# Expert queue: row number and expert change of two tiles packed in one word for SyncE, landing waits grouped, padding tiles counted as no change

## The chip, the cores and the metric

The kernel runs on one core of one Trainium2 chip. The metric is device time in microseconds (us), the median of several executions. A profiled execution comes with it: its span runs from the first to the last instruction of the program.

## The reference

A small language-model tower over 8 sequences of 512 tokens, 256 channels. The last of its three parts is the one that the change touches.

```python
h = _L0_tok_ref(x, ...)                       # embedding, depthwise convolution of 31 taps
h = h + _L0_attn_ref(_layernorm(h), ...)      # linear attention, 16 heads
h = h + _L0_ffn_ref(_layernorm(h), ...)       # 8 experts, 4 of width 256 and 4 of width 512, top 2

# inside _L0_ffn_ref
topw, sel = jax.lax.top_k(jax.nn.sigmoid(xf @ router_w.T), 2)
h = jnp.square(jax.nn.relu(jnp.einsum('td,edw->tew', xf, W1e)))
y = jnp.einsum('tew,ewd->ted', h, W2e)
out = jnp.einsum('ted,te->td', y, combine)
```

Each token goes to two experts, and the two weighted results are added to its row of the output.

## The kernel before

The routing step writes each token's row (256 channels, weight, token number) twice into `queue_d`, a queue in HBM that has a stretch of rows for every expert. When all are counted, VectorE works out a table over tiles of 128 rows: 71 tiles (`TILES`), the experts of width 512 first. Experts have whole numbers of tiles, so that some rows of a last tile, and all rows of the last tiles of the table (padding tiles), are filler rows, which add to 128 spare rows of the output.

**The expert loop** (function `experts`) goes through the tiles in order. Tile j takes these steps:

- SyncE (SP) loads the tile's rows from HBM into one of 8 slots (`load`, L1712 to L1715). It reads the row number from the table with a register load (`value_load`, L1710).
- TensorE turns the rows (L1849), multiplies by the first weights (L1859), turns the squared activations (L1875) and multiplies by the second weights (L1859). ScalarE (ACT) and VectorE (DVE) take the results out of PSUM in between: x_hi L1760, x_lo L1805, relu L1765, act_w L1817, a_hi L1771, a_lo L1823.
- ScalarE takes the result to `y` (`take_y`, L1777), one of 4 buffers (`RING`). Before it writes, the add of tile j - 4 from the same buffer must have landed. ScalarE works in order: while this instruction waits, all that comes after it waits.
- SyncE allows the add (`allow`, L1717 to L1727): it waits for y, then for landings of the adds of tiles j - 3 to j - 1, and increments `may_add`. If tile j belongs to another expert than tile j - 1, these three adds must have landed, since two experts may hold the same token. If not, the waits ask for one landing fewer of each buffer, which take_y has already waited for. The number to wait for is computed in a register from `apart`, a second table of 0 or 16.
- GpSimd (POOL) waits for `may_add` and issues the add as an indirect DMA that accumulates in `out` (L1748).

All engines but SyncE and GpSimd take the loop in turns of two tiles, with a branch at the head of each on whether its oldest tile is wide (L1698): wide tiles fall through, narrow ones jump. The expert numbers are read from a word for 8 tiles (L1695). `wait_apart` (L160 to L164) is a wait followed by an increment of a semaphore, `sp_passed`, that nobody waits for.

SyncE's queue is one program in order: for tile j it first does `load(j + 8)`, then `allow(j)`, and the next tile follows.

Of the kernel before, what the change touches and what calls it, by code (L numbers as in the profile page):

```python
# [23 lines left out]
I32 = mybir.dt.int32  # L24
U32 = mybir.dt.uint32
ALU = mybir.AluOpType
# [3 lines left out]
P = 128  # L30
# [33 lines left out]
EXPERTS = 8  # L64
# [5 lines left out]
TOPK = 2  # L70
QROWS = TOKENS + P
FILLER_ROW = EXPERTS * QROWS
ROW = DIM + 2

TILES = TOKENS * TOPK // P + EXPERTS - 1
# [2 lines left out]
SLOTS = 8  # L78
TABLE = -(-TILES // SLOTS) * SLOTS
FILLERS = TABLE - TOKENS * TOPK // P  # L80
TURN = 2
RING = 4
TOTAL_W = sum(WIDTHS)
# [34 lines left out]
class Dispatch:  # L118
# [3 lines left out]
    def __init__(self, sbuf, sem):  # L122
        self.filler = sbuf("filler", [P, ROW])
        self.filler_at = sbuf("filler_at", [P, FILLERS, 2], I32)
        self.count = sbuf("count", [P, EXPERTS])
        self.count_i = sbuf("count_i", [P, EXPERTS], I32)
        self.tiles = sbuf("tiles", [P, EXPERTS])
        self.upto = sbuf("upto", [P, EXPERTS, EXPERTS])
        self.end = sbuf("end", [P, EXPERTS])
        self.end_i = sbuf("end_i", [P, EXPERTS], I32)  # L130
        self.tile_no = sbuf("tile_no", [1, TABLE])
        self.row_of = sbuf("row_of", [1, TABLE], I32)
        self.word_of = sbuf("word_of", [1, TABLE // SLOTS], I32)

        self.apart = sbuf("apart", [1, TABLE], I32)
        self.consts, self.filler_ready, self.ends_ready, self.filled, self.chain, self.ready = (sem(n) for n in (
            "table_consts", "filler_ready", "ends_ready", "filled", "table_chain", "table_ready"))

# [21 lines left out]
def wait_apart(engine, sem, value, passed):  # L160


    engine.wait_ge(sem, value)
    engine.sem_inc(passed, 1)  # L164
# [477 lines left out]
def attend(nc, ctx, sem, bank, ident, base, base0, rw_t, w1, w2, h_d, store, h_in, loaded, h_stored, raw_in,  # L642
# [48 lines left out]
    before = sbuf("before", [P, P], BF16)  # L691
# [353 lines left out]
    def vector(dve):  # L1045
# [272 lines left out]
        n = [0]  # L1318

        def chained(ins):  # L1320

            n[0] += 1
            ins.then_inc(table.chain, 1)
            dve.wait_ge(table.chain, n[0])
# [3 lines left out]
        space, at = x2_t[:].rearrange("p k n -> p (k n)"), [0]  # L1328

        def taken(rows, n):  # L1330
# [5 lines left out]
        expert_f, start_f, differs = (taken(1, TABLE) for _ in range(3))  # L1336
# [20 lines left out]
                                        ALU.mult))  # L1357
        chained(nc.vector.tensor_reduce(start_f, passed, AX, ALU.add))
        chained(nc.vector.tensor_tensor(start_f, table.tile_no[:], start_f, ALU.subtract))
        chained(nc.vector.tensor_scalar(start_f, start_f, float(P), None, ALU.mult))  # L1360
        chained(nc.vector.scalar_tensor_tensor(out=start_f, in0=expert_f, scalar=float(QROWS), in1=start_f,
                                            op0=ALU.mult, op1=ALU.add))
        chained(nc.vector.tensor_copy(table.row_of[:], start_f))

        chained(nc.vector.memset(differs[:, 0:1], 0.0))
        chained(nc.vector.tensor_tensor(differs[:, 1:], expert_f[:, 1:], expert_f[:, 0:TABLE - 1], ALU.not_equal))
        chained(nc.vector.tensor_scalar(table.apart[:], differs, 16.0, None, ALU.mult))
        chained(nc.vector.tensor_scalar(expert_f, expert_f, float(EXPERTS - 1), None, ALU.min))

        pairs = expert_f.rearrange("p (n u) -> p n u", u=2)  # L1370
        chained(nc.vector.scalar_tensor_tensor(out=word2, in0=pairs[:, :, 1], scalar=float(EXPERTS),
                                               in1=pairs[:, :, 0], op0=ALU.mult, op1=ALU.add))
        pairs = word2.rearrange("p (n u) -> p n u", u=2)
        chained(nc.vector.scalar_tensor_tensor(out=word4, in0=pairs[:, :, 1], scalar=float(EXPERTS ** 2),
                                               in1=pairs[:, :, 0], op0=ALU.mult, op1=ALU.add))
# [270 lines left out]
def experts(nc, ctx, sem, bank, ident, store, table, queue_d, out, w1_parts, w1_lo_ready, w1_zero, w2_split, queued,  # L1646
            stored):
    def sbuf(name, shape, dt=F32):
        return ctx.enter_context(nc.sbuf_tensor(name, shape, dt))
# [54 lines left out]
    def sync(sp):  # L1704
        sp.wait_ge(table.ready, 1)
        attention_left(sp)


        def row_at(j):
            return sp.value_load(table.row_of[0:1, j:j + 1], min_val=0, max_val=FILLER_ROW + (FILLERS - 1) * P)  # L1710

        def load(j, at):  # L1712
            if j >= SLOTS:
                sp.wait_ge(row_used, j - SLOTS + 1)
            sp.dma_start(rows[:, j % SLOTS], queue_d[bass.ds(at, P), :]).then_inc(rows_in[j % SLOTS], 16)  # L1715

        def allow(j):  # L1717

            sp.wait_ge(y_ready, j + 1)
            if j >= RING:  # L1720
                differs16 = sp.value_load(table.apart[0:1, j:j + 1], min_val=0, max_val=16)
            for before in range(max(0, j - RING + 1), j):
                if before < RING:
                    sp.wait_ge(added[before % RING], 16)
                else:
                    wait_apart(sp, added[before % RING], differs16 + 16 * (before // RING), sp_passed)
            sp.sem_inc(may_add, 1)  # L1727

        first_rows = [row_at(j) for j in range(SLOTS)]
        sp.wait_ge(table.filled, 16 * (EXPERTS + 3))  # L1730
        sp.wait_ge(queued, 16 * TOPK * TT * BATCHES)
        for j in range(SLOTS):
            load(j, first_rows[j])
        for j in range(TILES):
            if j + SLOTS < TILES:
                load(j + SLOTS, row_at(j + SLOTS))
            allow(j)

    def gpsimd(pool):
        attention_left(pool)  # L1740
# [202 lines left out]
```

## Time and profile before

| | us |
|---|---|
| median of 3 executions | 714.23 (714.22 to 716.38) |
| profiled execution, its own time | 714.98 |
| span of the profiled execution | 713.3 |
| first add of the expert loop starts | 500.33 |
| last of its 71 adds starts | 705.40 |

About 1.7 us of the profiled execution's own time lie outside its span. TensorE is busy for 89% of the span, GpSimd for 45%. Starts in the rows are microseconds from the start of the span. The adds are numbered 0 to 70 in order of time, so that the last one is tile 70. The idle time of an engine that is not the bound costs nothing; what matters is who ends the wait of the engine that is late.

### The profile page before, as it was taken

Reading aid. Unit: us, or ns where it says so; the run is one execution under the profiler, and the core shown is the slowest. Engines: PE = TensorE matmul, PEld = TensorE weight load, DVE = VectorE, ACT = ScalarE, POOL = GpSimd, SP = SyncE. Lnnn points to the kernel's source line nnn. Section 1 sums busy time; section 2 is a strip of 40 time slices with the busy share of each in tenths; the row PEclk is TensorE's granted clock in tenths of the full one; section 3 lists DMA queues with packets and bytes.
Section 4 is the critical chain, followed back from the end, with each engine's and each line's share of the span. In section 5 each row is a group of like instructions: output and inputs, shape, how many; then the busy total and the mean of one; then the engine's idle time right before and its main releaser. Section 6 shows DMA issues by size and latency. Waiting matters only on the chain.

```text
span 713.3 us, 15773 instructions
## 1 busy us (share of the span) xinstructions
PE 631.3 (89%) x5032; PEld 546.0 (77%) x5032; DVE 468.4 (66%) x1219; ACT 306.8 (43%) x669; POOL 321.1 (45%) x292
## 2 busy tenths in 40 slices
PE   6988479999999999999999999615999999988881
PEld 6988357788887887878878787504999999888781
DVE  6466494877879778797897866764444555554450
ACT  2560135334453353633535327422545555555551
POOL 6340351330833717427165171752354544476574
PEclk9999698999999999999999999856999999999996
DMA  6550982010111201102010020423355445576664
GB/s 225 190 124 7 230 301 62 2 59 2 61 60 39 82 1 60 60 24 97 1 61 31 17 75 3 169 93 101 62 87 80 78 76 83 79 116 108 107 100 45
DMA packets 37215, 58.11 MB, mean 81 GB/s; under 512 B 5726, under 2 KB 31066, under 8 KB 36506
## 3 DMA queue, kind: packets, MB, share of 16 engines
q1 hardware_dynamic: 21282, 35.08, 16.9%
q0 software_dynamic: 14160, 20.13, 15.7%
q10 hardware_dynamic: 1672, 1.57, 0.7%
q8 instruction: 61, 1.00, 0.6%
q14 instruction: 40, 0.33, 0.2%
HBM read 28.30 MB, written 27.42 MB: 78 GB/s over the span
## 4 chain that ended last, share of the span: by engine, by line
PE 77%; DMA 8%; DVE 6%; issue 3%; POOL 2%; ACT 1%; SPq 1%; DVEq 0%; ACTq 0%; POOLq 0%
PE bank L1427 26%; PE bank L1859 16%; PE bank L1500 7%; DMA out<-y,token_at 7%; PE bank L1470 5%; PE bank L1456 4%; PE bank L1875 2%; PE bank L1488 2%; PE bank L546 2%; PE bank L547 2%; PE bank L567 2%; PE bank L1849 2%; PE bank L529 1%; PE bank L1418 1%; PE bank L1556 1%
## 5 line engine op out<-in xcount | busy, mean ns | idle before, releaser
L1748 POOL DMA_INDIRECT out<-y,token_at x71 | 111.8, 1575 | 108.3 <-SPq L1727 107.1
L886 POOL DMA_INDIRECT queue_d<-row,slot x56 | 59.7, 1066 | 129.0 <-DVE slot L1253 114.2
L1817 DVE SCALAR_TENSOR_TENSOR act_w<-relu,queue_rows 128x512 f32<-128x512 f32 (+1 forms) x71 | 44.6, 628 | 98.2 <-ACT relu L1765 52.0
L1427 PE MATMUL bank<-xt_hi,w_first 128*128 128x512 f32 x256 | 94.8, 416 | 0.9 <-DVE second_half L1091 0.9
L1427 PE MATMUL bank<-w_first,xt_hi 128*128 128x512 f32 x256 | 84.7, 412 | 3.1 <-DVE xt_lo L1081 2.3
L877 POOL TENSOR_TENSOR second_half<-second_half,q_inv 128x512 f32<-128x512 f32 x64 | 64.9, 1042 | 42.0 <-DVE q_inv L1100 41.9
L945 ACT ACTIVATE k_exps<-bank,k_negmax 128x512 f32<-128x512 f32 x64 | 44.2, 691 | 73.8 <-DVE k_negmax L1107 73.6
L937 ACT ACTIVATE second_half<-second_half 128x512 f32<-128x512 f32 x64 | 40.3, 632 | 74.3 <-DVE second_half L1091 74.3
L1859 PE MATMUL bank<-w_hi,a_hi 128*128 x214 | 65.9, 308 | 0.8 <-issue 0.5
L1427 PEld LDWEIGHTS bank<-w_first,xt_hi 128*128 128x128 f32 x256 | 46.2, 192 | 19.6 <-issue 6.8
L1859 PE MATMUL bank<-w_lo,a_hi 128*128 x214 | 59.8, 280 | 0.0
L1859 PE MATMUL bank<-w_hi,a_lo 128*128 x214 | 59.5, 278 | 0.0
L1765 ACT ACTIVATE relu<-bank 128x512 f32<-128x512 f32 (+1 forms) x71 | 35.3, 498 | 55.6 <-PE bank L1859 55.5
L1427 PEld LDWEIGHTS bank<-xt_hi,w_first 128*128 128x128 f32 x256 | 49.2, 192 | 11.0 <-DVE second_half L1091 1.8
L1088 DVE TENSOR_REDUCE q_max<-bank 128x8 f32<-128x512 f32 x64 | 42.0, 656 | 17.6 <-PE bank L1427 17.6
L1107 DVE TENSOR_REDUCE k_negmax<-bank 128x1 f32<-128x512 f32 x64 | 42.8, 679 | 14.8 <-PE bank L1427 13.8
L1427 PE MATMUL bank<-w_first,xt_lo 128*128 128x512 f32 x128 | 50.8, 397 | 0.0
L1427 PE MATMUL bank<-xt_lo,w_first 128*128 128x512 f32 x128 | 50.7, 396 | 0.0
L1500 PE MATMUL bank<-g,wv_t 128*128 128x256 f32 x224 | 49.5, 379 | 0.0
L1859 PE MATMUL bank<-w_first,x_hi 128*128 x142 | 39.7, 361 | 9.9 <-DVE x_lo L1805 4.4
L1777 ACT ACTIVATE y<-bank 128x256 f32<-128x256 f32 x71 | 27.4, 385 | 46.1 <-PE bank L1859 29.1
L1500 PEld LDWEIGHTS bank<-g,wv_t 128*128 128x128 f32 x224 | 42.5, 190 | 6.0
(201 smaller groups left out, 1583.8 us busy)
## 6 DMA issues: line engine op xcount, KB each, us to landing
queue_rows<-queue_d SPq DMA_DIRECT2D x71, 129.0 KB, 2.1
store<-in_L_ffn_w SPq DMA_DIRECT2D x4, 1536.0 KB, 8.6
out<-res SPq DMA_DIRECT2D x8, 512.0 KB, 2.9
h_d<-store SPq DMA_DIRECT2D x6, 512.0 KB, 9.0
h_in<-h_d SPq DMA_DIRECT2D x6, 512.0 KB, 4.1
windows<-taps_d SPq DMA_DIRECT2D x4, 512.0 KB, 5.8
wqk<-in_L_attn_w_qkv SPq DMA_DIRECT2D x1, 2048.0 KB, 13.5
out<-y,token_at POOLq DMA_INDIRECT x71, 4.0
```

The costliest lines, as they stand in the source:

```text
L877: nc.gpsimd.tensor_tensor(v, v, q_inv[:, b.par, u].unsqueeze(2).to_broadcast([P, 8, DH]), ALU.mult).then_inc(q_ready, 1)
L886: pool.indirect_dma_start(out=queue_d, in_=row_of(b)[:, t, c, :], in_offset=None, out_offset=bass.IndirectOffsetOnAxis(ap=slot[:, TT * c + ...
L937: nc.scalar.activation(v, v, ACT.Exp, scale=SCALE).then_inc(q_exp_ready, 1)
L945: nc.scalar.activation(k_exps[:, c % 2], qk_bank(10 + c)[:], ACT.Exp, bias=k_negmax[:, c:c + 1], accum_out=k_sum[:, b.par, c:c + 1]).then_ ...
L1088: link(nc.vector.tensor_reduce(q_max[:, u % 2], src, AX, ALU.max), q_chain, b, Q_LINKS, 2 * u + 1 - (u > 0))
L1107: nc.vector.tensor_reduce(k_negmax[:, c:c + 1], qk_bank(10 + c)[:], AX, ALU.max, negate=True).then_inc(k_max_ready, 1)
L1427: last = nc.tensor.matmul(o, a, c, start=(n == 1), stop=(n == 3 * len(pairs)))
L1470: last = nc.tensor.matmul(tail_bank(n)[DH * r:DH * r + DH, DH * a:DH * a + DH], k[:, t, c:c + DH], q[:, b.par, t, d:d + DH], start=(t == 0 ...
L1500: last = nc.tensor.matmul(tail_bank(6)[:, DIM * kk:DIM * kk + DIM], wv_t[:, a, P * kk:P * kk + P], g[:, a], start=(a == 0), stop=(a == PAI ...
L1748: pool.indirect_dma_start(out=out, in_=y[:, j % RING, :], in_offset=None, compute_op=ALU.add, out_offset=bass.IndirectOffsetOnAxis(ap=toke ...
L1817: nc.vector.scalar_tensor_tensor(out=act_w[:, u % 2, 0:width], in0=relu[:, u % 2, 0:width], scalar=rows[:, u, DIM:DIM + 1], in1=relu[:, u ...
L1859: last = nc.tensor.matmul(o, a, c, start=(n == 1), stop=(n == parts))
```

## The change

The table has one word for two tiles (`step_of`, 36 words) in place of `row_of` and `apart`. A word holds for each tile 9 bits for the number of its 128 rows in the queue and one bit for the change of expert. SyncE reads a word in every other pass, and takes the fields out with shifts and masks in registers. VectorE's chain loses three small instructions (times 128, copy to `row_of`, `apart`) and gains two (the two packings). The limit of the expert number to 7 comes before the comparison of neighbours, so that a step from the last expert to padding is no change. In `allow`, the waits of the three landings are grouped by the number that they wait for, with at most one increment of `sp_passed` between the groups in place of one after each wait.

```diff
-        chained(nc.vector.tensor_scalar(start_f, start_f, float(P), None, ALU.mult))
-        chained(nc.vector.scalar_tensor_tensor(out=start_f, in0=expert_f, scalar=float(QROWS), in1=start_f,
+        chained(nc.vector.scalar_tensor_tensor(out=start_f, in0=expert_f, scalar=float(QROWS // P), in1=start_f,
                                             op0=ALU.mult, op1=ALU.add))
-        chained(nc.vector.tensor_copy(table.row_of[:], start_f))
+        chained(nc.vector.tensor_scalar(expert_f, expert_f, float(EXPERTS - 1), None, ALU.min))
 
         chained(nc.vector.memset(differs[:, 0:1], 0.0))
         chained(nc.vector.tensor_tensor(differs[:, 1:], expert_f[:, 1:], expert_f[:, 0:TABLE - 1], ALU.not_equal))
-        chained(nc.vector.tensor_scalar(table.apart[:], differs, 16.0, None, ALU.mult))
-        chained(nc.vector.tensor_scalar(expert_f, expert_f, float(EXPERTS - 1), None, ALU.min))
+        chained(nc.vector.scalar_tensor_tensor(out=start_f, in0=differs, scalar=float(2 ** ROW_BITS), in1=start_f,
+                                            op0=ALU.mult, op1=ALU.add))
+        pairs = start_f.rearrange("p (n u) -> p n u", u=STEPS)
+        chained(nc.vector.scalar_tensor_tensor(out=table.step_of[:], in0=pairs[:, :, 1], scalar=float(2 ** STEP_BITS),
+                                               in1=pairs[:, :, 0], op0=ALU.mult, op1=ALU.add))
...
-        def row_at(j):
-            return sp.value_load(table.row_of[0:1, j:j + 1], min_val=0, max_val=FILLER_ROW + (FILLERS - 1) * P)
-
-        def load(j, at):
+        def steps_from(j):
+
+            n = j // STEPS
+            return sp.value_load(table.step_of[0:1, n:n + 1], min_val=0, max_val=2 ** (STEPS * STEP_BITS) - 1)
+
+        def load(j, steps):
             if j >= SLOTS:
                 sp.wait_ge(row_used, j - SLOTS + 1)
-            sp.dma_start(rows[:, j % SLOTS], queue_d[bass.ds(at, P), :]).then_inc(rows_in[j % SLOTS], 16)
-
-        def allow(j):
-
+            at = (steps >> (STEP_BITS * (j % STEPS))) & (2 ** ROW_BITS - 1)
+            at = nc.s_assert_within(at, 0, LAST_TILE, skip_runtime_bounds_check_because="the table numbers queue_d's tiles")
+            sp.dma_start(rows[:, j % SLOTS], queue_d[bass.ds(at * P, P), :]).then_inc(rows_in[j % SLOTS], 16)
+
+        def wait_landed(tiles, turn, apart16):
+
+            for b in tiles:
+                if b // RING == turn:
+                    sp.wait_ge(added[b % RING], apart16 + 16 * turn if turn > 0 else 16)
+
+        def allow(j, steps):
+
+            apart16 = (steps >> (STEP_BITS * (j % STEPS) + ROW_BITS - 4)) & 16
+            earlier = range(max(0, j - RING + 1), j)
             sp.wait_ge(y_ready, j + 1)
-            if j >= RING:
-                differs16 = sp.value_load(table.apart[0:1, j:j + 1], min_val=0, max_val=16)
-            for before in range(max(0, j - RING + 1), j):
-                if before < RING:
-                    sp.wait_ge(added[before % RING], 16)
-                else:
-                    wait_apart(sp, added[before % RING], differs16 + 16 * (before // RING), sp_passed)
+            if earlier and earlier[0] // RING < (j - 1) // RING:
+                wait_landed(earlier, earlier[0] // RING, apart16)
+                sp.sem_inc(sp_passed, 1)
+            if earlier:
+                wait_landed(earlier, (j - 1) // RING, apart16)
             sp.sem_inc(may_add, 1)
 
-        first_rows = [row_at(j) for j in range(SLOTS)]
+        words = [steps_from(j) for j in range(0, SLOTS, STEPS)]
         sp.wait_ge(table.filled, 16 * (EXPERTS + 3))
         sp.wait_ge(queued, 16 * TOPK * TT * BATCHES)
         for j in range(SLOTS):
-            load(j, first_rows[j])
+            load(j, words[j // STEPS])
         for j in range(TILES):
             if j + SLOTS < TILES:
-                load(j + SLOTS, row_at(j + SLOTS))
-            allow(j)
+                if j % STEPS == 0:
+                    words.append(steps_from(j + SLOTS))
+                load(j + SLOTS, words[(j + SLOTS) // STEPS])
+            allow(j, words[j // STEPS])
```

## Rows read from the trace of the kernel before

**Rows 1.** Two stretches of the expert loop: length, busy time of each engine.

```profile
core 0: us, PE busy (x) PEld busy (x) DVE busy (x) ACT busy (x) POOL busy (x), PEclk, DMA share, GB/s
500.00:618.00 118.00, 118.00 (x825) 107.33 (x824) 59.25 (x136) 59.88 (x137) 53.72 (x35) 1.00 0.49 79
618.00:660.00 42.00, 37.22 (x303) 35.21 (x301) 22.35 (x72) 23.98 (x74) 26.50 (x17) 1.00 0.67 107
```

**Rows 2.** Timeline of POOL: adds of tiles 35, 36, 44, 45, 68 to 70.

```profile
621.74 1.55 POOL L1748 DMA_INDIRECT out<-y,token_at  x1 [2.36 <-SPq L1727]
625.90 1.80 POOL L1748 DMA_INDIRECT out<-y,token_at  x1 [2.61 <-SPq L1727]
...
642.60 1.56 POOL L1748 DMA_INDIRECT out<-y,token_at  x1 [0.80 <-SPq L1727]
647.83 1.55 POOL L1748 DMA_INDIRECT out<-y,token_at  x1 [3.67 <-SPq L1727]
...
699.49 1.56 POOL L1748 DMA_INDIRECT out<-y,token_at  x1 [0.30 <-issue]
703.54 1.55 POOL L1748 DMA_INDIRECT out<-y,token_at  x1 [2.49 <-SPq L1727]
705.40 1.56 POOL L1748 DMA_INDIRECT out<-y,token_at  x1 [0.30 <-issue]
```

**Rows 3.** Chain of work over one SyncE pass: start, us, what.

```profile
635.95 0.27 SPq L1710
...
636.52 0.04 SPq L1715
...
637.07 0.27 SPq L1721
...
637.62 0.04 SPq L163
...
637.70 0.02 SPq L164
...
638.24 3.97 DMA out<-y,token_at
```

**Rows 4.** The add's line from 618 us on: who waited; time to landing.

```profile
  ACT y L1777: 16.9, 13
...
DMA to landing us min/median/max: 3.7/4.1/5.3
```

**Rows 5.** Timeline of PE: first weight product of tiles 40, 46, 48, 64, 70.

```profile
624.36 0.38 PE L1859 MATMUL bank<-w_first,x_hi 128*128 x1 [1.10 <-DVE x_lo L1805]
...
637.60 0.38 PE L1859 MATMUL bank<-w_first,x_hi 128*128 x1 [0.47 <-DVE x_lo L1805]
...
642.47 0.38 PE L1859 MATMUL bank<-w_first,x_hi 128*128 x1 [0.92 <-DVE x_lo L1805]
...
681.38 0.38 PE L1859 MATMUL bank<-w_first,x_hi 128*128 x1 [1.33 <-issue]
...
694.35 0.38 PE L1859 MATMUL bank<-w_first,x_hi 128*128 x1 [0.36 <-DVE act_w L1817]
```

**Rows 6.** The loop's branch line: its compare-and-branch on PE's queue, ns min/median/max.

```profile
L1698 PEldq COMPARE_BRANCH  x56: 68/208/442, 489.8 to 697.6; - x56
```

**Rows 7.** Timeline of ACT: y of tiles 35, 44, 49, 68.

```profile
619.65 0.38 ACT L1777 ACTIVATE y<-bank 128x256 f32<-128x256 f32 x1 [0.67 <-PE bank L1859]
...
639.75 0.38 ACT L1777 ACTIVATE y<-bank 128x256 f32<-128x256 f32 x1 [0.20 <-PE bank L1859]
...
652.18 0.39 ACT L1777 ACTIVATE y<-bank 128x256 f32<-128x256 f32 x1 [1.76 <-DMA out<-y,token_at]
...
696.29 0.38 ACT L1777 ACTIVATE y<-bank 128x256 f32<-128x256 f32 x1 [0.27 <-PE bank L1859]
```

**Rows 8.** Waits of SyncE's queue: who for whom, us, times, longest.

```profile
SPq L1731 <- DMA queue_d<-k,slot: 0.7, 1, 0.7
```

**Rows 9.** Waits from 470 to 510 us, same columns.

```profile
PE bank L1849 <- DMA queue_rows<-queue_d: 17.5, 1, 17.5
```

More of the change, by code:

```diff
@@ L72 @@
 FILLER_ROW = EXPERTS * QROWS
+STEPS = 2
+ROW_BITS = 9
+STEP_BITS = ROW_BITS + 1
 ROW = DIM + 2
@@ L80 @@
 FILLERS = TABLE - TOKENS * TOPK // P
+LAST_TILE = (FILLER_ROW + FILLERS * P) // P - 1
 TURN = 2
@@ L131, in __init__ @@
         self.tile_no = sbuf("tile_no", [1, TABLE])
-        self.row_of = sbuf("row_of", [1, TABLE], I32)
+        self.step_of = sbuf("step_of", [1, TABLE // STEPS], I32)
         self.word_of = sbuf("word_of", [1, TABLE // SLOTS], I32)
-        self.apart = sbuf("apart", [1, TABLE], I32)
         self.consts, self.filler_ready, self.ends_ready, self.filled, self.chain, self.ready = (sem(n) for n in (
```

## The prediction

> **What bounds the kernel now.** I read the busy time by stretch first, then the timeline of the adds, then the chain of work through one SyncE pass, then the waits of ScalarE and the pace of TensorE.
>
> The expert loop has two stages. In the wide one, 500 to 618 us, TensorE is busy without a gap, 118.00 of 118.00 us [rows 1]; nothing that SyncE does there can change the time. In the narrow one the bound changes hands. TensorE is busy 37.22 of 42.00 us [rows 1], and ScalarE's y waits for landed adds for 16.9 us in 13 places [rows 4]. The adds run late: the first narrow ones go out up to 4 us after their y. The last add starts at 705.40 [rows 2], and some 8 us after it (landing, drain) are the same in both kernels. So the question is when the last add can start.
>
> Three things hold the adds. (a) SyncE's pass. From the read of the row number at 635.95 to that of the next tile it does these pieces, with ends read off the starts of the next [rows 3]: row word 635.91 to 636.52, 0.61; row load to 637.07, 0.55; read of `apart` to 637.62, 0.55; register add and three waits with their increments to 637.98 (the add's start less 0.27), 0.36. That is 2.07 us, and narrow adds in full flow follow at that distance, while GpSimd alone manages 1.86, as 703.54 to 705.40 shows [rows 2]. (b) A change of expert, where the add waits for the one before to land: 621.74 to 625.90 (4.16) and 642.60 to 647.83 (5.22) are two of five, at tiles 36, 45, 51, 57 and 69, of 4.16, 5.22, 4.44, 4.39 and 4.05; I take the median, 4.39. (c) The last of these, tile 69, is the step to padding: 699.49 to 703.54, 4.05 [rows 2].
>
> **Part 1: padding is no change.** Tile 69 follows tile 68 by 1.86 in place of 4.05: 2.19 less, all on the path, since nothing but adds is left there.
>
> **Part 2: SyncE's pass.** Removed: the read of `apart`, 0.55 in each pass, and the read of the row word in every other, 0.61 / 2 = 0.31. Added: shift and mask for the row and for the bit, four register operations. The nearest row is the register add, 637.62 to the next at 637.70, 0.08 each [rows 3]: 0.32. The increments of `sp_passed` save about 0.05. Pass: 2.07 - 0.55 - 0.31 + 0.32 - 0.05 = 1.48, below GpSimd's 1.86, so GpSimd sets the pace of adds. Bounds: at nothing for the fields the pass is 1.2 (no other pace); at the 0.2 that a register piece takes behind a load (what is left of 0.55 after the 0.27 of the load, halved or so) it is about 2.0 (no gain of pace).
>
> From y to its add the shortest path before is the piece from 637.07 to 638.24, 1.17 [rows 3]. Without the read and with two operations it is 1.17 - 0.55 + 0.16 - 0.05, some 0.7. Behind the waiting instruction in SyncE's queue stands load(j + 9), which is used six tiles later, and is not missed.
>
> **What TensorE allows.** Once the adds are early, y is not held, and TensorE's own pace is the floor. Unheld it is seen from tile 40 to tile 48: 624.36 to 642.47, 18.11 for eight tiles: three pairs in 13.24 (to 637.60) and one, with the read of the next word, in 4.87 [rows 5]. It is not all matmuls: TensorE sat idle 0.47 before the product at 637.60, and the x_lo that the row names is the next tile's, its own was done a tile earlier. What takes this time is the jump to the narrow branch, 0.44 at its longest on TensorE's queue [rows 6], with the instructions behind it. Tile 70 unheld would start at 624.36 + 3 x 18.11 + 13.24 = 691.93; it started at 694.35 [rows 5], so all the holding costs TensorE only 2.42. The 16.9 us of waits [rows 4] are mostly swallowed: a hold of 1.76 at tile 49 [rows 7] made no pair late.
>
> The rule in the Trainium skill, page Advanced Engine Details and Errata, section Control Flow Timing, is about 108 ns for a compare-and-branch. The trace doesn't agree for TensorE's jump (0.44). By the page's figure a pair would be 0.33 shorter, TensorE no longer the floor at the end, and the time, as an estimate, 705.8.
>
> **The sum, along the adds** (y's end is its row plus 0.38).
>
> - Tile 35: y 619.65 + 0.38 + 0.7 = 620.73, before 621.74 [rows 2, 7].
> - Tile 36, a change: + 4.16 = 624.89.
> - Tile 44: adds alone 624.89 + 8 x 1.86 = 639.77; its y 639.75 + 0.38 + 0.7 = 640.83 [rows 7]. TensorE decides.
> - Tile 45, a change: + 4.39 = 645.22. Tile 50: + 5 x 1.86 = 654.52. Tile 51, a change: 658.91. Tile 56: 668.21. Tile 57, a change: 672.60. Tile 68 by adds alone: 672.60 + 11 x 1.86 = 693.06.
> - Is y held behind a change? y of tile 49 needs the landing of 45, 645.22 + 4.1 [rows 4] = 649.3; unheld it starts at 650.9 (tile 50's product at 642.47 + 4.4 = 646.9, tile 51's 1.95 later, and y of a tile starts 2.1 after the product two tiles on, as 637.60 and 639.75 show [rows 5, 7]). The same for 55 (663.0 against 664.5) and 61 (676.7 against 677.8). Not held.
> - Tile 68 by TensorE: y 696.29 - 2.42 + 0.38 = 694.25, + 0.7 = 694.95 [rows 7]. This is later than 693.06, so TensorE decides.
> - Tiles 69 and 70: + 2 x 1.86 = 698.67. Before 705.40: 6.73 less.
>
> As parts: 2.42 from TensorE unheld, 2.12 from the path from y to add at tile 68 (2.82 to 0.7), 2.19 from padding.
>
> **Part 3: the start.** VectorE's chain is one small instruction shorter. It is covered: after the table SyncE makes eight reads of 0.61 each, now four, and then still waits 0.7 for the last queue write [rows 8]. If that write came earlier, fewer reads would be a gain. Behind that wait TensorE waits for the first row load [rows 9], and the first two loads now have their field operations before them: 0.08 to 0.3 later, I take 0.15, and the wide stage passes it on whole.
>
> 6.73 - 0.15 = 6.6 less. Against the profiled execution: span 706.7, its own time 714.98 - 6.6 = 708.4. That execution lies 0.75 above the median, so for the median 714.23 - 6.6 = 707.6.
>
> **Fast end.** From tile 64 to 70, 681.38 to 694.35 [rows 5], the pairs took 4.32 on average. With these, eight tiles are 3 x 4.32 + 4.87 = 17.83, tile 70 starts at 690.82, and the last add at 697.6; with 0.5 in place of 0.7 behind y, 697.4: 706.4.
>
> **Rivals.**
>
> *Landings get longer.* Adds at 1.86 put more on HBM per us than at 2.07, and landings already reach 5.3 [rows 4]. With 5.3 + 0.36 at each change: tile 36 at 626.4, 45 at 646.9, 51 at 661.9, 57 at 676.9; y of tile 61 is held to 682.2 in place of 677.8, 4.4, of which 1.8 are swallowed, so TensorE is 2.6 late; last add 701.3, time 710.3. For it: the median is 4.1 and some already take 5.3, with nothing else to see. Against it: in the tail, where adds follow by 1.86, tile 68's landed within 4.05 [rows 2]. The Trainium skill (DMA: Bandwidth & Descriptors, Latency and other measured facts) has the completion cost grow with HBM load; of growth with the pace of adds the trace shows neither.
>
> *The pass stays at 2.03.* The fields cost what the reads did. Then tile 57 at 674.6, 62 at 684.8, the six after it (their passes have no load) at 1.86, last add 699.6: 708.6. Inside the range.
>
> *Only padding gains*, since the adds wait for something else than SyncE: 714.2 - 2.2 = 712.0. Against it: GpSimd sits 0.45 idle before most narrow adds until SyncE's increment, and in the tail, where the pass has no row load, it doesn't.
>
> *Slower: register work.* If fields, limits and addresses recompute more than seen here, the pass exceeds 2.07. It must pass 2.3 before 21 tiles of excess eat padding's and TensorE's share: register work of 1.15 us in place of 0.32, over a dozen operations at 0.08. At 2.5 the time is 718. Nothing in the rows has so many.
>
> **Chances.** The sum (706.4 to 709), 0.64; landings longer (709 to 711.5), 0.13; pass at 2.03, 0.08; padding alone, 0.06, half of it over the bound; no change for another reason, 0.04; slower, 0.05. A measurement here tells 0.3%, 2.1 us, from no change. Faster 0.64 + 0.13 + 0.08 + 0.03 = 0.88, same 0.07, slower 0.05. Range 706.4 to 710.8.
>
> **What the profile after should show.** `step_of` read 36 times by SyncE and no read of `apart`; adds within an expert 1.86 apart after a change, then 2.2 to 2.3 where they have caught up with y; y to add 0.7 there; ScalarE's waits for landings near 0 in place of 16.9; tile 70's product near 692; tile 69 1.86 behind 68; TensorE's wide stage as it was. The prediction is wrong if TensorE's pairs change (by a faster or slower branch), if landings after changes take over 5, or if SyncE's even passes, with the read, run over 2.

## The result: 1.1% faster, and the profile after

The changed kernel took 707.33 us, the median of 4 executions (706.74 to 710.09), against 715.31 for the kernel before with the executions of the same series (714.22 to 716.51). The ratio is 0.9893, 95% interval 0.9864 to 0.9922. The forecast was 707.6, 0.92% less than the median it started from.

The profiled execution took 710.09 and has a span of 708.4: it is the slowest of the four, and why is part of the story. Here is the timeline of its adds, tiles 35, 36, 44 to 46 and 68 to 70, as in [rows 2]:

```profile
622.35 1.55 POOL L1764 DMA_INDIRECT out<-y,token_at  x1 [1.78 <-SPq L1741]
626.82 1.56 POOL L1764 DMA_INDIRECT out<-y,token_at  x1 [2.91 <-SPq L1741]
...
642.72 1.56 POOL L1764 DMA_INDIRECT out<-y,token_at  x1 [0.91 <-SPq L1741]
646.88 1.56 POOL L1764 DMA_INDIRECT out<-y,token_at  x1 [2.61 <-SPq L1741]
648.74 1.56 POOL L1764 DMA_INDIRECT out<-y,token_at  x1 [0.30 <-issue]
...
696.82 1.56 POOL L1764 DMA_INDIRECT out<-y,token_at  x1 [0.90 <-SPq L1741]
698.68 1.55 POOL L1764 DMA_INDIRECT out<-y,token_at  x1 [0.30 <-issue]
700.54 1.56 POOL L1764 DMA_INDIRECT out<-y,token_at  x1 [0.30 <-issue]
```

Behind a change of expert the next add comes 1.86 later, and its engine was kept by nobody ("issue", 0.30): SyncE had allowed it by then. Tile 69 follows 68 by 1.86 as well, where the step to padding took 4.05. Tile 68's add, in contrast, waited 0.90 for SyncE, and SyncE for y.

TensorE's timeline, first products of tiles 8, 40, 46, 48, 64 and 70, as in [rows 5]:

```profile
517.73 0.50 PE L1875 MATMUL bank<-w_first,x_hi 128*128 x1
...
626.27 0.38 PE L1875 MATMUL bank<-w_first,x_hi 128*128 x1 [1.23 <-issue]
...
639.59 0.38 PE L1875 MATMUL bank<-w_first,x_hi 128*128 x1 [0.45 <-DVE x_lo L1821]
...
644.45 0.38 PE L1875 MATMUL bank<-w_first,x_hi 128*128 x1 [0.92 <-DVE x_lo L1821]
...
680.63 0.38 PE L1875 MATMUL bank<-w_first,x_hi 128*128 x1 [1.08 <-DVE x_lo L1821]
...
693.59 0.38 PE L1875 MATMUL bank<-w_first,x_hi 128*128 x1 [0.34 <-issue]
```

Tile 40 to 48 takes 18.18, as before (18.11); 40 to 70 takes 67.32 in place of 70.00. TensorE's free pace now holds to the end. ScalarE's y says the same, from 618 us on (who ended the idle time before it: us, times), where [rows 4] had 16.9 us in 13 places:

```profile
its engine sat idle before it (us, times) until:
  PE bank L1875: 10.0, 36
  DMA out<-y,token_at: 0.3, 1
...
```

SyncE's queue, by line (ns min/median/max): 36 word reads, and the register operations of the loads (L1723) and of the waits (L1729):

```profile
L1716 SPq TENSOR_LOAD <-step_of x36: 262/268/535, 479.9 to 680.4; - x36
```

```profile
L1723 SPq ALU_OP  x106: 32/37/51, 485.7 to 681.0; - x106
```

```profile
L1729 SPq ALU_OP  x230: 32/37/46, 520.8 to 699.1; - x115
```

Since the start of the loop moves from run to run, I use one length for all that follows: **from the first product of tile 8 to the start of the last add**. Before: 516.18 to 705.40, 189.22. After: 517.73 to 700.54, 182.81, which is 6.41 less. The forecast for this stretch was 6.73 less.

### The profile page after: what moved, and what is told of

The parts are those of the page before. It is cut to its first block, busy times and chain, and to the rows that moved or that the text cites. A ratio compares the mean times of both kernels' runs of the same rounds, so it can differ in the third digit from the quotient of the medians.

```text
span 708.4 us, 15575 instructions
## 1 busy us (share of the span) xinstructions
PE 631.5 (89%) x5032; PEld 546.8 (77%) x5032; DVE 468.0 (66%) x1218; ACT 308.0 (43%) x669; POOL 320.6 (45%) x292
## 3 DMA queue, kind: packets, MB, share of 16 engines
q1 hardware_dynamic: 21282, 35.08, 16.9%
## 4 chain that ended last, share of the span: by engine, by line
PE 82%; DVE 8%; issue 3%; POOL 2%; DMA 2%; ACT 2%; SPq 0%; DVEq 0%; POOLq 0%
PE bank L1431 26%; PE bank L1875 21%; PE bank L1504 7%; PE bank L1474 5%; PE bank L1460 4%; PE bank L1891 3%; PE bank L1492 2%; PE bank L548 2%; PE bank L549 2%; PE bank L569 2%; PE bank L1865 2%; PE bank L531 1%; PE bank L1422 1%; DVE act_w L1833 1%; PE bank L1560 1%
## 5 line engine op out<-in xcount | busy, mean ns | idle before, releaser
L1093 DVE TENSOR_TENSOR second_half<-bank,q_max 128x512 f32<-128x512 f32 x64 | 44.3, 692 | 2.2
```

Of the source, the lines that this page charges most:

```text
L1093: nc.vector.tensor_tensor(v, src, q_max[:, u % 2].unsqueeze(2).to_broadcast([P, 8, DH]), ALU.subtract).then_inc(q_shifted, 1)
```

## The experiments

The kernel before took 725.7 in the first of the three series, 715.1 in the second and 715.4 in the third, each on another chip. The difference lies ahead of the loop, whose first product starts at 498.3 to 499.6 in the profiles of the first series and at 487.1 to 493.2 in the others. So each row gives its ratio to the kernel before in the same series, and the length of the loop as defined above. Spacing is the median distance of the adds of tiles 37 to 62, the changes of expert left out. "Held" is how long ScalarE's y waited for landings from tile 36 on.

```
kernel              time    ratio (95%)              loop    tiles 40-70  spacing  held
before              714.98  (profiled)               189.22  70.00        2.05     16.9
before_again        714.92  one execution            190.23  71.01        2.07     13.9
pad_only            723.49  0.9972 (0.9954-0.9991)   187.02  70.23        2.07     16.0
group_only          710.20  0.9935 (0.9903-0.9966)   187.67  69.40        1.95     10.2
packed_only         710.65  0.9949 (0.9922-0.9975)   185.63  68.00        1.86      1.2
pad_waits           711.54  0.9949 (0.9927-0.9970)   184.97  67.52        1.86      0.4
after               707.33  0.9893 (0.9864-0.9922)   182.81  67.32        1.86      0.3
after_again         718.97  0.9904 (0.9873-0.9934)   182.60  67.22        1.86      0.0
read_behind_y       719.89  0.9921 (0.9896-0.9946)   184.22  68.02        2.00      2.7
read_in_load        711.98  0.9944 (0.9913-0.9975)   185.12  68.55        2.02      6.7
two_reads_in_load   735.09  1.0130 (1.0095-1.0166)   199.78  82.78        2.71     23.0
swap                709.98  0.9927 (0.9896-0.9958)   183.42  68.31        1.86      0.8
turn4               720.36  1.0064 (1.0035-1.0094)   196.03  76.37        1.88      1.5
words_first         705.91  0.9865 (0.9840-0.9889)   179.98  65.58        1.86      3.2
```

Two of the eleven executions of `swap`, of 1068.50 and 3504.69 us, lie far from the other nine (708.19 to 714.09) and are not in its ratio; nothing on record tells what happened in them.

### Both kernels once more

`after_again` and `before_again` have no edit.

> The changed kernel once more, for a second profile and a closer ratio. The first profile of it took 710.09 us while its three other executions took 706.74 to 707.65; its loop from the first weight product of tile 8 (517.73) to the last add (700.54) took 182.81, against 189.22 before (516.18 to 705.40), 6.41 less, but it reached tile 8 1.55 us late. If that late start is the change's own (field operations in front of the first loads), this profile has it again: tile 2's product some 6.2 us after tile 0's, and an own time near 710. If it is chance (how long TensorE stayed at its lower clock), tile 2 follows tile 0 by some 5.2 and the own time is near 707. The loop from tile 8 takes 182.8 within 0.5 in both.

> The kernel before once more, for a second profile. So far tile 2's product followed tile 0's by 5.2 us in three profiles and by 6.2 in five, with either kind of load, and I take it for chance. Loop from the first product of tile 8 to the last add 189.2 within 0.7; if it is 187.7 as in the run with grouped waits alone, that run's 1.5 us were scatter from run to run and not the grouping.

The late start was in the second profile of the changed kernel too (tile 2's product 6.19 after tile 0's), but it is not the change's: it was in the second profile of the kernel before (6.34), and not in three kernels that have the changed loads, `two_reads_in_load` (5.21), `read_behind_y` (5.23) and `swap` (5.28). What differs is TensorE's clock. Stretches of the start of the loop, with busy times, then granted clock, DMA share and GB/s, first of the first profile before, then of the second:

```profile
491.00:493.00 2.00, 2.00 (x7) 1.45 (x6) 2.00 (x2) 0.01 (x1) 0.00 (x0) 0.50 0.16 52
493.00:495.20 2.20, 2.20 (x14) 1.86 (x12) 1.73 (x4) 1.27 (x3) 0.00 (x0) 0.95 0.00 0
```

```profile
488.50:490.80 2.30, 2.30 (x8) 1.71 (x7) 2.30 (x2) 0.01 (x1) 0.00 (x0) 0.50 0.27 79
490.80:493.50 2.70, 2.70 (x8) 2.06 (x7) 1.72 (x4) 0.86 (x2) 0.00 (x0) 0.50 0.04 7
493.50:496.00 2.50, 2.50 (x17) 2.14 (x16) 1.59 (x4) 1.51 (x4) 0.00 (x0) 0.97 0.14 45
```

The first product started at 490.04 and 487.84. In the one the grant of the full clock (0.95 to 1, of the level of 2.4 GHz) came some 3 us after it, in the other some 5.7. While it is 0.50 (1.2 GHz) TensorE is as busy, and does half. The kernel is the same; this is 1.0 to 1.2 us of chance in every execution. The loop from tile 8, which begins after that, was 190.23 in `before_again` against 189.22, so loops of one kernel can differ by about 1. The 187.67 of the run with grouped waits alone lies 1.55 under the lower of these two.

### Padding alone

`pad_only`, on the kernel before:

```diff
+        chained(nc.vector.tensor_scalar(expert_f, expert_f, float(EXPERTS - 1), None, ALU.min))
         chained(nc.vector.memset(differs[:, 0:1], 0.0))
         chained(nc.vector.tensor_tensor(differs[:, 1:], expert_f[:, 1:], expert_f[:, 0:TABLE - 1], ALU.not_equal))
         chained(nc.vector.tensor_scalar(table.apart[:], differs, 16.0, None, ALU.mult))
-        chained(nc.vector.tensor_scalar(expert_f, expert_f, float(EXPERTS - 1), None, ALU.min))
```

> The kernel before with the third part of the change alone: the expert number is limited before neighbours are compared, so that padding is no change. My theory: the last change of 4.05 becomes a plain 1.86 to 2.07, so the loop from tile 8 to the last add takes 189.22 - 2.2 = 187.0, and the time is 2.2 us less, ratio 0.997. Rival (padding was never on the path, all came from SyncE's pass): no change. Rival (padding was most of it): 5 us or more.

Loop 187.02, 2.20 less than in the first profile before, ratio 0.9972 with an interval that leaves out 1. Since loops differ by about 1 from profile to profile, the firmer reading is the gap itself: tile 69's add follows 68's by 1.86 here, against 4.05 and 4.15 in the two profiles before. As expected by my theory.

### Everything but padding, the word alone, the grouping alone

`pad_waits` (the changed kernel, limit behind the comparison):

```diff
-        chained(nc.vector.tensor_scalar(expert_f, expert_f, float(EXPERTS - 1), None, ALU.min))
         chained(nc.vector.memset(differs[:, 0:1], 0.0))
         chained(nc.vector.tensor_tensor(differs[:, 1:], expert_f[:, 1:], expert_f[:, 0:TABLE - 1], ALU.not_equal))
+        chained(nc.vector.tensor_scalar(expert_f, expert_f, float(EXPERTS - 1), None, ALU.min))
```

> The changed kernel, but the step to padding counts as a change of expert again. My theory (the parts add up, since padding comes after all that the rest touches): loop from tile 8 182.7 + 2.2 = 184.9, of tile 69's gap alone. Rival (landing and grouping interact): 183.5 or less.

`packed_only` has that edit, and in `allow` the waits of the kernel before:

```diff
-            if earlier and earlier[0] // RING < (j - 1) // RING:
-                wait_landed(earlier, earlier[0] // RING, apart16)
-                sp.sem_inc(sp_passed, 1)
-            if earlier:
-                wait_landed(earlier, (j - 1) // RING, apart16)
+            for before in earlier:
+                if before < RING:
+                    sp.wait_ge(added[before % RING], 16)
+                else:
+                    wait_apart(sp, added[before % RING], apart16 + 16 * (before // RING), sp_passed)
```

> The kernel before with the packed word alone: padding counts as a change, and each landing wait is followed by its increment as before. The kernel before takes 189.2 in the loop from tile 8, the one with everything but padding should take 184.9. If grouping is worth about nothing once the reads are gone (my theory, since the pass is then below the pace of TensorE): 184.9 to 185.3. Rival (grouping is worth the 1.5 us that its run alone showed, whatever else): 186.4.

`group_only`, on the kernel before:

```diff
-            for before in range(max(0, j - RING + 1), j):
-                if before < RING:
-                    sp.wait_ge(added[before % RING], 16)
-                else:
-                    wait_apart(sp, added[before % RING], differs16 + 16 * (before // RING), sp_passed)
+            earlier = range(max(0, j - RING + 1), j)
+            for turn in sorted({b // RING for b in earlier}):
+                for b in earlier:
+                    if b // RING == turn:
+                        sp.wait_ge(added[b % RING], differs16 + 16 * turn if turn > 0 else 16)
+                if turn != (j - 1) // RING:
+                    sp.sem_inc(sp_passed, 1)
```

> The kernel before with only the waits of the landings grouped by their limit, so that there are fewer increments of the semaphore that nobody waits for. My theory: an increment rides on the wait that is there anyway, and the pass goes from 2.07 to 2.0 at the least; the loop from tile 8 takes 189.2 within 1, no change of time. Rival (the increments were dear): pass 1.9, loop 186 or less.

The kernel without the padding part took 184.97, the expected 184.9: the parts add up. The word alone took 185.63, between the two theories (185.3 and 186.4) but nearer to mine; it has adds at 1.86 already, so the word, not the grouping, frees SyncE. It also met a slow landing (5.40 at tile 57, against 4.20 in `pad_waits`). The grouping alone brought the spacing from 2.05 to 1.95 and the loop to 187.67, more than I gave it (no change) and less than its rival (186). It is below both loops of the kernel before, and the time is less too, 0.9935 with an interval that excludes 1. So where SyncE's pass is the bound, the grouping pays; where the reads are gone, what is left of it (185.63 to 184.97) is within the scatter.

One thing does not fit. The ratio of `group_only` stands for 4.6 us less (2.4 to 6.9), its loop for 1.5 to 2.6 less. What the rest is stays open. By the ratios alone the grouping would even be worth as much as everything but padding (0.9935 against 0.9949); the loops (187.67 against 184.97) say otherwise. Ratios with intervals of 0.3% on either side can't rank parts of this size, and I go by the loops.

### Putting reads back: how long may SyncE's pass be?

`read_in_load` has the first added line; `two_reads_in_load` has it twice; `read_behind_y` has the second added line. The values are not used.

```diff
         def load(j, steps):
             if j >= SLOTS:
+                sp.value_load(table.word_of[0:1, 0:1], min_val=0, max_val=EXPERTS ** SLOTS - 1)
                 sp.wait_ge(row_used, j - SLOTS + 1)
...
             sp.wait_ge(y_ready, j + 1)
+            sp.value_load(table.word_of[0:1, 0:1], min_val=0, max_val=EXPERTS ** SLOTS - 1)
```

> The changed kernel with two unused register reads in each load from tile 8 on, ahead of its wait. SyncE's pass in the changed kernel is 1.0 without and 1.55 with a word, 1.3 on average; two reads add 1.2, so 2.5 on average, more than GpSimd's 1.86 and TensorE's 2.27. My theory (the pass bounds the adds as soon as it is over those): adds of narrow tiles up to 62 are 2.5 apart, the last add some 11 us later than in the changed kernel, the time about 718, slower than the kernel before. Rival (SyncE's pass is not what spaced the adds): within 1 us of the changed kernel, 707.5.

> The changed kernel with one unused register read in each load, ahead of the waits of load and allow. Pass 1.3 + 0.6 = 1.9 on average, y to add unchanged at 0.7. With two reads the loop took 199.8, with one behind the wait for y 184.2, without 182.7. My theory (the average pass must be under TensorE's pace of 2.27 per tile, and near GpSimd's 1.86 only after a change of expert): adds after a change 2.0 apart, loop 183.2, 0.5 more. Rival (it is the reads as such, wherever they stand): 184.2 as with the read behind y.

> The changed kernel with one unused register read in each allow, behind the wait for y, where the kernel before read its second table. The pass is 1.3 + 0.6 = 1.9 on average, no more than GpSimd's own 1.86 within the noise, so the pace stays; but the path from y to the add grows from 0.7 to 1.25. My theory, in which TensorE sets y at the end and the add follows it: the last add 0.5 to 1.0 us later, time 708.2. Rival (the pass must keep up in each tile, not on average): the passes with a word take 2.15, and the loss is 3 us or more. Rival (path from y to add plays no part): 0.

Two reads made the kernel slower than before, 1.013. That SyncE's pass can bound the loop is thus shown from both sides. The loss, 17 us, was larger than the 11 expected: adds are 2.71 apart, not 2.5, and the row loads, which sit in the same queue, come late. The waits of this kernel from 618 us on (us, times, longest):

```profile
ACT y L1795 <- DMA out<-y,token_at: 23.0, 17, 3.0
...
PEld bank L1867 <- DMA queue_rows<-queue_d: 11.8, 10, 2.6
```

One read cost 1.5 in the loop behind the wait for y, where I had expected 0.5 to 1.0, and 2.4 ahead of it, where I had expected 0.5. Both expectations missed. The difference of 0.9 between the two is no more than two profiles of one kernel differ by, so no effect of the position is shown; what the two have in common is the spacing of 2.0. I had asked that the pass be under TensorE's 2.27 per tile, and took 2.0 for harmless. It is not: after each change of expert the adds are about 3 us behind and have to catch up before the next change, and they catch up by 0.4 per tile at 1.86 but by a bit over 0.2 at 2.0. With 6 tiles between changes that decides whether they arrive. The traces agree: the add of tile 50, the last before a change, starts 0.75 after the end of its y in the changed kernel, and 2.03 and 1.96 after it in `read_behind_y` and `read_in_load`. The add of tile 51, behind the change, is then 5.07 and 4.67 late in place of 3.67.

### TensorE's floor: the branch

`swap` on the changed kernel:

```diff
-            with engine.If(((words[oldest // SLOTS] >> (3 * (oldest % SLOTS))) & (EXPERTS - 1)) < WIDE):
+            with engine.If(((words[oldest // SLOTS] >> (3 * (oldest % SLOTS))) & (EXPERTS - 1)) >= WIDE):
                 for j in range(first, first + TURN):
-                    step(words, j // SLOTS, j % SLOTS, MAXW)
+                    step(words, j // SLOTS, j % SLOTS, NARROW_W)
             with engine.Else():
                 for j in range(first, first + TURN):
-                    step(words, j // SLOTS, j % SLOTS, NARROW_W)
+                    step(words, j // SLOTS, j % SLOTS, MAXW)
```

> The changed kernel with the two branches of the loop exchanged on TensorE, ScalarE and VectorE: narrow turns fall through, wide ones jump. In the changed kernel tile 70's first product follows tile 40's by 67.3, in pairs of 4.4 (3.77 without TensorE's idle time at the head of a turn). Theory 1 (the long jump from the head into the narrow branch is what costs): narrow pairs take 4.0, tiles 40 to 70 take some 62, the adds' own chain becomes the bound, the loop from tile 8 to the last add takes 181 in place of 182.7, ratio to the kernel before 0.987 to 0.989. Theory 2 (any taken jump over that much code costs, and a narrow turn now ends with one over the wide branch): pairs stay 4.4, no change. In both the wide stage keeps its 3.43 per tile, since its matmuls are long enough to cover a jump.

`turn4`:

```diff
-TURN = 2
+TURN = 4
```

> The changed kernel with turns of four tiles in place of two, so half the branches; the first narrow turn then begins at tile 40 in place of 38, two tiles more at full width cost some 3.2 us. If the branch is what holds TensorE in narrow turns (0.6 to 0.7 for each), tiles 40 to 70 take 67.3 - 7 x 0.65 = 62.8, and TensorE reaches tile 70 1.3 us earlier in all; the last add 1 to 1.5 us earlier, loop from tile 8 some 181.5. If TensorE's narrow pace has another cause, tiles 40 to 70 stay at 67 and the loop takes 186, 3.2 more.

Exchanging the branches changed nothing to the good: tiles 40 to 70 took 68.31. That is theory 2, a jump over the other branch has to be taken somewhere. In `swap` from 620 us on TensorE's queue has two branches per narrow turn, one of 0.08 that falls through and, at the end of the turn's code, one of 0.18 to 0.39. (The changed kernel has the same pair in the wide stage, 0.07 and 0.17 to 0.31, so wide turns jump too; there TensorE's products have no gap.)

`turn4` missed both expectations by far: loop 196.03, where I had 181.5 or 186. It has half the branches, but some are much longer. The branch line on TensorE's queue, ns min/median/max, of the changed kernel and of `turn4`:

```profile
L1702 PEldq COMPARE_BRANCH  x56: 67/192/442, 490.3 to 696.8; - x56
```

```profile
L1702 PEldq COMPARE_BRANCH  x29: 68/284/2827, 487.5 to 706.9; - x29
```

With two tiles' code to pass a jump took at most 0.44 us. With four tiles' code, five of the eight jumps into narrow turns from 620 us on took 1.04 to 2.83, the other three 0.33 to 0.34; what tells them apart is open. The longest stands ahead of tile 48's product in `turn4`'s timeline of PE:

```profile
646.78 0.58 PE L1875 MATMUL bank<-w_first,x_hi 128*128 x1 [3.42 <-issue]
```

Jumps are not all of the loss. In two more places, ahead of the products at 659.48 and 699.47, TensorE sat idle in the middle of a turn, from 1.7 us after the end of the last branch on and with no wait that the profile shows. They are the second line here, of the waits from 626 us on (us, times, longest):

```profile
PE bank L1875 <- issue: 8.1, 4, 3.4
PE bank L1891 <- issue: 4.2, 2, 2.1
```

Besides, tiles 38 and 39 at full width cost 3.7, as far as tile 40's product tells (112.20 after tile 8's, against 108.54).

Neither run makes the instruction stream shorter, and neither by itself shows that the stream is what idles TensorE at the head of a narrow turn. The row of tile 48 names x_lo of VectorE. The changed kernel's trace settles it: the last x_lo ahead of that product ended at 643.71, and TensorE's queue was taken all the while, with the read of the expert word from 643.01 on (0.30, then 0.15 and 0.02 for two operations that belong to it), with two register operations and with the branch of 0.23, which ended at 644.09. A wait and two more register operations fill the time to the product at 644.45.

```profile
643.30 0.41 DVE L1821 TENSOR_TENSOR x_lo<-bank,x_hi 128x256 fp32r<-128x256 f32 x1
```

```profile
L1699 PEldq TENSOR_LOAD <-word_of x1: 302/302/302, 643.0 to 643.0; - x1
```

```profile
L1702 PEldq COMPARE_BRANCH  x1: 229/229/229, 643.9 to 643.9; - x1
```

### A version that beats both: the words read ahead

If TensorE is the floor, its reads of the expert words, one at every fourth turn, are on the path. `words_first` does all nine while the three engines wait for the first rows:

```diff
+    def all_words(engine):
+        return [engine.value_load(table.word_of[0:1, n:n + 1], min_val=0, max_val=EXPERTS ** SLOTS - 1)
+                for n in range(TABLE // SLOTS)]
...
-            if first % SLOTS == 0 and first < TILES:
-                words.append(engine.value_load(table.word_of[0:1, first // SLOTS:first // SLOTS + 1], min_val=0,
-                                               max_val=EXPERTS ** SLOTS - 1))
...
-        x_turn(0, 0, 0, 0)
-        x_turn(1, 1, 1, 0)
         pe.wait_ge(table.ready, 1)
+        words = all_words(pe)
+        x_turn(0, 0, 0, 0)
+        x_turn(1, 1, 1, 0)
```

and so on ScalarE and VectorE, ahead of their first x_high and x_low. The run thus takes the reads off three engines at once; that TensorE's are the ones that count rests on the queue above.

> The changed kernel, in which TensorE, ScalarE and VectorE read all nine words of expert numbers while they wait for the first rows, in place of one at every fourth turn. In the changed kernel TensorE sets the end, at 4.4 per pair and 4.9 for a pair with such a read. If that is so, tiles 40 to 70 take 67.2 - 3 x 0.5 = 65.7, with 0.5 more before tile 40; the adds' own chain then begins to bind, so the last add comes 1.2 to 1.9 us earlier: loop from tile 8 181.1, time 0.2% under the changed kernel, 0.988 of the kernel before. Rival (the adds' chain was the bound all along): loop unchanged at 182.7.

Tiles 40, 48 and 70 in its timeline of PE, then the last add in that of POOL:

```profile
623.74 0.38 PE L1877 MATMUL bank<-w_first,x_hi 128*128 x1 [0.36 <-DVE x_lo L1822]
...
641.22 0.38 PE L1877 MATMUL bank<-w_first,x_hi 128*128 x1 [0.28 <-DVE x_lo L1822]
...
689.32 0.38 PE L1877 MATMUL bank<-w_first,x_hi 128*128 x1 [0.35 <-issue]
```

```profile
696.29 1.56 POOL L1764 DMA_INDIRECT out<-y,token_at  x1 [0.30 <-issue]
```

Tiles 40 to 70 take 65.58 (65.7 expected), and TensorE's idle time ahead of tile 48 is 0.28 in place of 0.92. The loop is 179.98, 2.7 less than the 182.7 of the changed kernel, more than the 1.6 I gave it, since tile 40 also came earlier (107.43 after tile 8, against 108.54). The time is 705.91, ratio 0.9865, against 0.9893 and 0.9904. The intervals of these ratios overlap, so that this version beats the kernel before is sure; that it beats the changed one rests on its trace.

## Why the prediction was right

Along its own steps, each relative to tile 8's product in the two profiles:

- **TensorE unheld, forecast 2.42**: tile 70's product came 178.17 after tile 8's before and 175.86 after, 2.31 less. The floor was the right one: 40 to 48 took the same 18.1 in both, and words read ahead moved it as it should.
- **y to add, forecast 2.12 (2.82 to 0.7)**: 2.82 before, 0.92 after at tile 68, 1.90 less. In the wide stage it was 0.6 to 0.7.
- **Padding, forecast 2.19**: 2.19 in the profile, 2.20 in the run that had it alone.
- **The pass, forecast 1.48, under GpSimd's 1.86**: adds after a change are 1.86 apart, kept by nobody. From one row load to the next, where nothing held the queue, the changed kernel took 1.05 to 1.12 in a pass without the word and 1.62 to 1.71 in one with it, some 1.4 on average. The field operations have the price of a row of before: 37 ns each, about 0.08 with the gap. I priced the grouping's share too low. With the reads still there it brought the spacing down by 0.1, not 0.05, and the loop by 1.5 or more.
- **Holds of y swallowed**: from 16.9 to 0.3, as forecast near 0.
- **The start, forecast 0.15, mis-sized**: it costs 0.7. The chain of work at the start of the loop in the changed kernel:

```profile
485.61 0.02 SPq L1745
...
485.94 2.26 DMA queue_rows<-queue_d
```

The first load is issued 0.33 after the wait, in place of 0.21, as I had said. But the second is issued at 487.1, 1.54 after the wait, in place of 0.79: the row below, of the load line alone between 486.5 and 487.2, has its register operation at 486.9, half a microsecond after the one before it.

```profile
L1723 SPq ALU_OP  x1: 37/37/37, 486.9 to 486.9; - x1
```

All ten profiles with the packed word have 1.54 or 1.55 there, all four with the old table 0.78 or 0.79, so it is the new code and no chance. TensorE needs tile 1's rows before it goes on; its first product came 4.2 to 4.5 after SyncE's wait in the kernels with the old table, and 4.9 to 5.1 with the packed word (4.4 in `words_first`, where TensorE has no word to read at that point). The wide stage passes this on whole. Why SyncE stands still between two register operations there is open.

The sum of the measured parts is 2.31 + 1.90 + 2.19 - 0.7 = 5.7 for a mean execution. The measured ratio, taken on 715.31, is 7.7 us with an interval of 5.6 to 9.7; that of `after_again` 0.9904, 6.9. The loops say the same from their side: 189.7 on average before and 182.7 after, 7.0 less, minus 0.7 is 6.3.

The mechanism was right, and each of the three large terms was met to 0.25 or better. That the median came out 0.3 from the forecast is more than that, and in part luck: the kernel before took 715.31 in the series of the result where the forecast started from 714.23, and the start, mis-sized by 0.55, is hidden in the width of the interval.

The rivals: landings did not get longer at the closer spacing. From 618 us on they took:

```profile
DMA to landing us min/median/max: 3.8/4.1/5.2
```

against 3.7/4.1/5.3 [rows 4]. The growth of the completion cost with HBM load, which the Trainium skill gives (DMA: Bandwidth & Descriptors, Latency and other measured facts), does not show between adds 2.07 and 1.86 apart. That the pass stays at 2.0 was made by hand in two runs: it gives back 1.5 to 2.4 of the gain in the loop, where I had worked out 1.0 (708.6 against 707.6). The prediction's estimate of 705.8 had a slip: with pairs 0.33 shorter tile 44 comes earlier too, its add follows the adds alone (639.77), and the same sum gives 704.7. Nothing rests on it. The slower rival was made by hand too, with a pass above 2.3, and did come out slower than the kernel before.

## What to carry to other kernels

A queue engine that computes nothing can still set the pace: add up one pass through its program, register reads included, and compare it with the engine that it serves; here 0.55 us for a register read, and two of them per tile, stood against an add that takes 1.86. The limit that such a pass must keep is not the mean pace of the slowest engine: where something throws the queue back now and then, it must be short enough to catch up before the next such event. And once it is, ask at once who is next: here TensorE's own instruction stream, whose register reads could be done while it waited for its first data.

## What the runs showed of the hardware

- A compare-and-branch on TensorE's queue took 0.07 us where it falls through and 0.17 to 0.44 where it jumps over two tiles' code; with four tiles' code it took 0.19 to 2.83. On ScalarE the same branch took 0.03 to 0.05. In the wide stage TensorE's products have no gap at jumps of 0.17 to 0.31; in the narrow one they do. The figure of the Trainium skill, some 108 ns (Advanced Engine Details and Errata, Control Flow Timing), lies between the two ends of the changed kernel and is no guide for a jump on TensorE.
- In the first microseconds of the loop the full TensorE clock was granted some 3 us after the first product in some executions and some 5.7 in others of the same program, which moves all that follows by 1.0 to 1.2 us.
- A register read on SyncE, 0.27 at the median, took up to 0.565 in the kernel before (L1721) and 0.623 in `group_only` (L1710). Its whole piece in the pass was 0.55 to 0.61 where the read was at its median.
